# A graph-network layer on one core: edge features and one-hot rows by DMA and ScalarE in place of TensorE, five z banks, all relative targets in one pass

## What is computed

```python
h = jnp.maximum(_layernorm(x, axis=-1), 0.0)
msg_in = jnp.concatenate([h[src], h[dst], edge_attr_32], axis=-1)
messages = act(msg_in @ W1 + b1) @ W2 + b2          # act is x * sigmoid(x)
att_logits = act(msg_in @ Wa1 + ba1) @ Wa2 + ba2
att = jax.nn.softmax(att_logits, axis=0)            # over all edges
messages = messages * att
aggregated = jax.ops.segment_sum(messages, dst, num_segments=6250)
upd_in = jnp.concatenate([h, aggregated], axis=-1)
out = x + act(upd_in @ Wu1 + bu1) @ Wu2 + bu2
```

## Time and profile before

| | |
|---|---|
| median of 3 runs | 2698.34 us (2697.96 to 2699.22) |
| span of the profiled execution | 2700.1 us |
| PE busy (matmul) | 1688.2 us, 63% |
| PE weight loads | 1368.1 us, 51% |
| DVE busy | 1364.4 us, 51% |
| ACT busy | 1064.0 us, 39% |
| POOL busy | 1660.9 us, 62% |
| DMA | 147.93 MB, mean 55 GB/s |
| mean granted TensorE clock | 0.627 of full speed |

### The profile page before, as it was taken

One profiled execution on the slowest core, in us unless ns is written; L12 is line 12 of the kernel. 1 busy time (PEld: TensorE's weight loads), 2 busy tenths in 40 slices (PEclk: granted clock), 3 DMA queues, 4 the chain that ended last, 5 costly groups with the idle time before them and its releaser, 6 DMA issues.

```text
span 2700.1 us, 33245 instructions
## 1 busy us (share of the span) xinstructions
PE 1688.2 (63%) x9168; PEld 1368.1 (51%) x9168; DVE 1364.4 (51%) x2976; ACT 1064.0 (39%) x1875; POOL 1660.9 (62%) x1630
## 2 busy tenths in 40 slices
PE   4366665665766555666666576556666656656668
PEld 3244454554555444554554465445555545545555
DVE  6154444454554445554455554445554445555465
ACT  3244334343434334344334344434344334334342
POOL 4466666566666666666666666666666666666630
PEclk8566667566576666666566655666665666666565
DMA  4221221112222221222222222221222222222200
GB/s 110 70 58 53 56 53 51 51 51 55 54 59 55 54 54 53 54 61 54 55 54 52 55 60 54 55 53 53 55 60 55 54 54 53 55 55 59 52 24 25
DMA packets 122692, 147.93 MB, mean 55 GB/s; under 512 B 66232, under 2 KB 86636, under 8 KB 122668
## 3 DMA queue, kind: packets, MB, share of 16 engines
q0 software_dynamic: 51584, 105.75, 15.1%
q1 hardware_dynamic: 61528, 37.81, 5.3%
q10 hardware_dynamic: 9556, 4.09, 0.5%
HBM read 139.52 MB, written 8.00 MB: 55 GB/s over the span
## 4 chain that ended last, share of the span: by engine, by line
PE 29%; another core or an unknown queue 25%; issue 24%; DVE 13%; ACT 6%; DVEq 1%; ACTq 1%; DMA 1%; SPq 0%
PE bank L631 10%; PE bank L639 8%; DVE s L853 4%; PE bank L615 4%; DVE z L875 2%; DVE z L855 2%; PE ps_prep L595 2%; ACT comb L466 2%; ACT bank L463 2%; PE bank L662 1%; ACT th L485 1%; DVEq L843 1%; PE bank L730 1%; DVE lg L857 1%
## 5 line engine op out<-in xcount | busy, mean ns | idle before, releaser
L374 POOL DMA_INDIRECT p_rows<-p_tab,src_i x1612 | 1640.8, 1018 | 936.1 <-issue 487.5
L631 PE MATMUL bank<-q_win,comb 128*128 128x128 f32 x3224 | 750.8, 396 | 268.8 <-issue 192.0
L631 PEld LDWEIGHTS bank<-q_win,comb 128*128 128x128 f32 x3224 | 656.6, 295 | 354.5 <-issue 257.0
L639 PE MATMUL bank<-hot,v 128*65 128x96 f32 x3224 | 496.8, 302 | 335.2 <-issue 329.1
L463 ACT ACTIVATE bank<-bank,row_no 96x512 f32<-96x512 f32 x403 | 255.9, 648 | 944.8 <-remote 595.6
L639 PEld LDWEIGHTS bank<-hot,v 128*65 128x65 f32 x3224 | 400.4, 177 | 397.1 <-issue 391.1
L853 DVE SCALAR_TENSOR_TENSOR s<-th,z 128x512 f32<-128x512 f32 x403 | 276.3, 686 | 297.4 <-ACT th L485 210.0
L846 DVE SCALAR_TENSOR_TENSOR acc<-acc,fade,bank 65x96 f32 x81 | 25.1, 310 | 743.5 <-remote 579.8
L485 ACT ACTIVATE th<-z 128x512 f32<-128x512 f32 x403 | 253.0, 628 | 260.9 <-DVE z L875 175.1
L875 DVE TENSOR_TENSOR z<-bank,p_rows 128x512 f32<-128x512 f32 x403 | 273.7, 679 | 128.9 <-remote 114.0
L615 PE MATMUL bank<-relT,sel 20*128 20x128 bf16 x1612 | 219.5, 279 | 147.9 <-issue 121.3
(11 more groups left out here) (129 smaller groups left out, 723.8 us busy)
## 6 DMA issues: line engine op xcount, KB each, us to landing
p_rows<-p_tab,src_i POOLq DMA_INDIRECT x1612
ef_sb<-edge_attr SPq DMA_DIRECT2D x80, 320.0 KB
q_win<-q_tab ACTq DMA_DIRECT2D x81, 48.0 KB
p_tab<-th SPq DMA_DIRECT2D x12, 256.0 KB, 2.3
q_tab<-th SPq DMA_DIRECT2D x12, 256.0 KB
x_sb<-x SPq DMA_DIRECT2D x3, 512.0 KB, 5.7
out<-s SPq DMA_DIRECT2D x12, 128.0 KB, 2.0
dst_i<-dst SPq DMA_DIRECT2D x80, 10.0 KB
```

The source lines that it names most:

```text
L374: pool.indirect_dma_start(p_rows[:, a, t * H2:(t + 1) * H2], None, p_tab, bass.IndirectOffsetOnAxis(src_i[:, a, t:t + 1], 0)).then_inc(gat ...
L631: last = nc.tensor.matmul(ps_z[(q + a) % 2][:, (t % TQ) * H2:(t % TQ + 1) * H2], comb[:, a, t * P:(t + 1) * P], q_win[:, a, :], start=True ...
L639: last = nc.tensor.matmul(ps_part[0:U1, 0:WIN], v[:, t, :], hot[:, a, t * WIN:(t + 1) * WIN], start=(t == 0), stop=(t == T - 1))
```

## The change

- The host lays out `src`, `dst` and the features: edge e of a tile lies on partition e (`src.reshape(-1, P).T`), and the features are transposed (`efT`).
- A DMA on SP brings the features straight into the lower 32 rows of `comb`. Another, `load_dst_b`, copies the targets of a group to 96 partitions (`dst_b`, one buffer, 96 x 2560 int32, 983 KB). ACT makes the one-hot by target from it in two parts of 1024 and 1536 columns, `Abs` and `Relu`, both in SBUF. `prepare`, `spread`, `copy_efT`, `copy_relT`, `sel` and `relT` go. The window load moves from ACT's queue to SP's.
- The bank of z is one per quarter (`ps_z = bank[0:5]`); `ps_part`, `ps_small` and the `units` product have banks of their own.
- PE's order for a group is now: the five `zmm` of the next group, each after `add_rows` of the same quarter of this group, then the two matmuls of the maximum, then all 20 of `sums`.
- `rel` of all groups is made once, before `q_rows`; DVE's `window` goes, and the check of the window is done at the start.
- `th` has two slots of a quarter; exp writes the weights into column 64 of `v`; `weigh` and the product of the logits are `scalar_tensor_tensor` (times 1.0) where they were `tensor_tensor`.

```diff
+        def load_window(eng, g, a):
+            node = eng.value_load(base_i[0:1, bass.ds(g, 1)], min_val=0, max_val=N - WIN)
+            eng.dma_start(q_win[0:WIN, a, :], q_tab[bass.ds(node, WIN), :]).then_inc(win_ld[a], 16)
+        def load_ef(eng, g, a, s):
+            T = tiles(g)
+            eng.dma_start(comb[WIN:P, a, 0:T * P], efT[:, bass.ds(g * GE, T * P)]).then_inc(s, 16)
+        def load_dst_b(eng, g):
+            T = tiles(g)
+            eng.dma_start(dst_b[:, 0:T * P], dst_row[:, bass.ds(g * GE, T * P)].broadcast_to([WIN, T * P])).then_inc(dst_b_ld, 16)
...
             def load_group(g, a):
-                wait(sp, prep_done, g - 1)
-                load_edges(sp, g, a, ld[a])
-                if not (isinstance(g, int) and g < 2):
-                    sp.wait_ge(gath[a][NQ - 1], per(a, g - 2, 16 * TQ))
-                load_src(sp, g, a, src_ld[a])
+                nxt, nxt2 = following(g)
+                if nxt is not None:
+                    sp.wait_ge(abs_ok, 2 * g + 2)
+                    load_dst_b(sp, nxt)
+                    wait(sp, z_done, g * NQ)
+                    if not (isinstance(nxt, int) and nxt < 2):
+                        load_ef(sp, nxt, 1 - a, ef_ld[1 - a])
+                    load_window(sp, nxt, 1 - a)
+                if nxt2 is not None:
+                    sp.wait_ge(gath[a][NQ - 1], per(a, g, 16 * TQ))
+                    load_src(sp, nxt2, a, src_ld[a])
...
             def zmm(g, a, q):
                 if q == 0:
-                    pe.wait_ge(efT_ok, g + 1)
+                    pe.wait_ge(ef_ld[a], per(a, g, 16))
                     pe.wait_ge(win_ld[a], per(a, g, 16))
-                wait(pe, z_ok, g * NQ + q - 1)
-                pe.wait_ge(comb_ok, g * NQ + q + 1)
+                wait(pe, z_ok, (g - 1) * NQ + q + 1)
+                if q in (0, 2):
+                    pe.wait_ge(comb_ok, 2 * g + 1 + q // 2)
...
             def group(g, a, units=False):
-                    spread(nxt, 1 - a, [2])
-                    zmm(g, a, 4)
-                    spread(nxt, 1 - a, [3])
-                    zmm(nxt, 1 - a, 0)
-                    spread(nxt, 1 - a, [4])
-                    zmm(nxt, 1 - a, 1)
+                if nxt is not None:
+                    for q in range(tiles(nxt) // TQ):
+                        zmm(nxt, 1 - a, q)
                 pe.wait_ge(pmax_ok, g + 1)
                 nc.tensor.transpose(ps_small[0:1, 0:P], pmax[:], ident[:]).then_inc(maxT_done, 1)
                 pe.wait_ge(gmax_ok, g + 1)
                 nc.tensor.matmul(ps_small[:, 0:1], ones[0:1, :], gmax[:], start=True, stop=True).then_inc(maxB_done, 1)
-                if nxt2 is not None:
-                    prepare(nxt2, a)
-                if nxt is not None:
-                    zmm(nxt, 1 - a, 2)
-                if nxt2 is not None:
-                    spread(nxt2, a, [0, 1])
                 pe.wait_ge(v_ok, g + 1)
                 pe.wait_ge(hot_ok, 2 * g + 2)
                 wait(pe, acc_ok, g)
-                sums(g, a, 0, TG // 2)
-                if nxt is not None and tiles(nxt) > 3 * TQ:
-                    zmm(nxt, 1 - a, 3)
-                sums(g, a, TG // 2, TG)
+                sums(g, a)
...
-                nc.vector.tensor_tensor(parts(z, q)[:, :, U:H2], parts(s2, q)[:, :, U:H2], wa2h[:].unsqueeze(1).broadcast_to([P, TQ, U]), ALU.mult).then_inc(s_sem, 1)
+                nc.vector.scalar_tensor_tensor(parts(z, q)[:, :, U:H2], parts(s2, q)[:, :, U:H2], 1.0, wa2h[:].unsqueeze(1).broadcast_to([P, TQ, U]),
+                                               ALU.mult, ALU.mult).then_inc(s_sem, 1)
...
-                return nc.vector.tensor_tensor(v[:, 0:T, 0:U], s2[:, 0:T, 0:U], ws[:, 0:T].unsqueeze(2).broadcast_to([P, T, U]), ALU.mult)
+                return nc.vector.scalar_tensor_tensor(v[:, 0:T, 0:U], s2[:, 0:T, 0:U], 1.0, w.unsqueeze(2).broadcast_to([P, T, U]), ALU.mult, ALU.mult)
```

More of the change, by code:

```diff
@@ L438, in _ @@
             batches(act, copy_h)
-            def window(g, a):
-                wait(act, z_done, (g - 1) * NQ)
-                node = act.value_load(base_i[0:1, bass.ds(g, 1)], min_val=0, max_val=N - WIN)
-                act.dma_start(q_win[0:WIN, a, :], q_tab[bass.ds(node, WIN), :]).then_inc(win_ld[a], 16)
-            def copy_efT(dst_a, T):
-                for j in range(TQ):
-                    last = nc.scalar.copy(comb[WIN:P, dst_a, 0:T * P].rearrange("p (q j e) -> p q j e", j=TQ, e=P)[:, :, j, :],
-                                          ps_prep[j * DE:(j + 1) * DE, 0:T * DE].rearrange("p (q e) -> p q e", e=P))
-                return last
@@ L469, in _, with one_hot_abs @@
-            stored(act, q_st)
-            act.wait_ge(base_ok, 1)
-            act.wait_ge(const_ok, 8)
-            window(0, 0)
-            copy_relT(0, 0)
-            copy_efT(0, TG).then_inc(efT_ok, 1)
-            for qs in ([0, 1], [2, 3], [4]):
-                one_hots(0, 0, qs)
-            copy_relT(1, 1)
+            HALF = [(0, 2 * TQ * P), (2 * TQ * P, TG * P)]
+            def one_hot_abs(g, a, k):
+                c0, c1 = HALF[k][0], min(HALF[k][1], tiles(g) * P)
+                if k == 0:
+                    act.wait_ge(dst_b_ld, 16 * (g + 1))
+                    wait(act, z_done, (g - 1) * NQ)
+                    act.sem_inc(turn, 1)
+                nc.scalar.activation(comb[0:WIN, a, c0:c1], dst_b[:, c0:c1], ACT.Abs, bias=row_of[0:WIN, bass.ds(g, 1)]).then_inc(abs_ok, 1)
@@ L479, in group, with one_hot_relu @@
+            def one_hot_relu(g, a, k):
+                c0, c1 = HALF[k][0], min(HALF[k][1], tiles(g) * P)
+                act.wait_ge(abs_ok, 2 * g + k + 1)
+                nc.scalar.activation(comb[0:WIN, a, c0:c1], comb[0:WIN, a, c0:c1], ACT.Relu, scale=-1.0, bias=ones[0:WIN, 0:1]).then_inc(comb_ok, 1)
+            act.wait_ge(const_ok, 7)
+            act.wait_ge(rel_ok, 1)
+            for k in range(2):
+                one_hot_abs(0, 0, k)
+                one_hot_relu(0, 0, k)
             def group(g, a, units=False):
-                nxt, nxt2 = following(g)
@@ L606, in spread @@
-            def spread(g, a, qs):
-                T = tiles(g)
-                for q in [q for q in qs if q < T // TQ]:
-                    if q == 0:
-                        pe.wait_ge(relT_ok, g + 1)
-                    wait(pe, comb_ok, g * NQ + q - 1)
-                    pe.sem_inc(turn, 1)
-                    for t in range(q * TQ, (q + 1) * TQ):
-                        last = nc.tensor.matmul(ps_row[(q + a) % 2][:, (t % TQ) * P:(t % TQ + 1) * P], sel[0:T, t, :], relT[0:T, :], start=True, stop=True)
-                    last.then_inc(row_done, 1)
@@ L1052 @@
     from concourse.bass_utils import run_bass_kernel_spmd
+    P = 128
+    GE = EDGE_TILES * P
+    full = N_EDGES // GE * GE
+    last = -(-(N_EDGES - full) // (4 * P)) * 4 * P
+    edges = np.concatenate([np.arange(full), np.arange(N_EDGES - last, N_EDGES)])
+    src, dst, ef = (np.ascontiguousarray(inputs[n])[edges] for n in ("src", "dst", "edge_attr_32"))
+    laid = {
+        "src": src.reshape(-1, P).T,
+        "dst": dst.reshape(-1, P).T,
+        "dst_row": dst.reshape(1, -1),
+        "efT": ef.T,
+    }
+    for name in _INS:
+        laid[name] = inputs[name]
     nc = bacc.Bacc("TRN2", target_bir_lowering=False, num_devices=1)
     arrays, args = {}, []
-    for name in _INS:
-        a = np.ascontiguousarray(inputs[name])
+    for name in ["x", "src", "dst", "dst_row", "efT"] + _INS[1:]:
+        a = np.ascontiguousarray(laid[name])
         arrays[name] = a
```

300 lines of the change are left out of this document (126 added, 174 removed).

## The result

| | before | after |
|---|---|---|
| median, us | 2698.15 (4 runs) | 2651.64 (4 runs) |
| span of the profiled execution, us | 2700.1 | 2645.8 |
| ratio of the times | 1 | 0.983 (95%: 0.981 to 0.985) |

The changed kernel is 1.7% faster; 6.6% was forecast. These are the page's rows of after that answer to the earlier trace rows: busy us, share and instructions by engine, then groups with busy us, mean ns, and idle us before them.

A forecast was written before the change was run, and what follows sets the result against it. POOL's gathers plus stops caused by PE's crawl were taken to bound the kernel. Gathers 25.5 + stops 3.6 = 29.1 us a group; 136 + 78.6 x 29.1 + 99 = 2522, median 2520 us (6.6% less), 8-in-10 range 2230 to 2700.

The forecast's parts named there:

- What bounds the kernel now: Edge groups: 31.3 us each, POOL working 26.4 and stopped 4.9, because PE crawls after some 81 records beside gathers.
- PE's work: PE per group: spreads and transposes go, 110 records become 84, so POOL stops less often.
- m: Groups between two stops of POOL: forecast 1.53, bounds 1 and no stop at all.
- Gathers: POOL's 20 gathers a group: scalar_tensor_tensor for tensor_tensor spares 0.9 us, 26.4 to 25.5; bounds 24.8 and 26.4.
- Stops: POOL's stops: 5.5 us each instead of 4.9, which per group is 3.6 us.
- Head and tail: Before and after the gathering groups: head unchanged at 136 us, give or take 6; tail from 102 to 99.
- ACT, DMAs, banks: ACT's passes, the added dst_b loads (6.1 us a group, covered) and the five z banks: no effect on the time.
- The sum: Whole kernel: 136 + 78.6 groups of 29.1 us + 99 = 2522 us of span, 2520 us median.
- one stop in each group: Rival for POOL: only gathers shrink, 30.4 us a group, 2622 us; chance 0.20.
- Slower: the maximum behind z: Rival at PE: the maximum waits behind 40 records of z, stops grow 5.2 to 10.1 us, 2756 us; chance 0.15.
- It changes nothing: Rival: gathers stay at 26.4 us with one stop of 4.9 a group, 2697 us; chance 0.06.
- POOL never stops: Rival: 84 records stay below what brings the crawl on, only POOL's 25.5 us a group remain, 2237 us; chance 0.17.

The follow-up runs named there:

- tt_back_c: Changed kernel with the logit product and v as tensor_tensor again, on a crawling chip: 2652.7 us, 0.983 of the kernel before.
- after_c: Changed kernel, unaltered, run again on a crawling chip: 2650.9 us, 0.982 of the kernel before.
- tt_back: Changed kernel with the logit product and v as tensor_tensor again, on a chip without the crawl: 2232.0 us, 0.989 of the kernel before.
- w_psum: Changed kernel, ACT writing the weights also into PSUM, where v reads them from group 14 on: 0.983 of before without the crawl (2209.4 us), 0.980 with it (2643.3).
- before_again: Kernel before, unaltered, traced on a chip without the crawl: 2246.0 us.
- after_again: Changed kernel, unaltered, on a chip without the crawl: 2233.5 us, 0.991 of the kernel before.
- max_first: Changed kernel with PE's records of the maximum ahead of the last two quarters of the next group's z, on a crawling chip: 2614.5 us, 0.971 of before.
- late_ahead: Changed kernel, add_part behind the partial maximum, next group's first z added before the wait for the maximum; no crawl: 2278.1 us, 1.008 of before.
- half_sums: Changed kernel without every second tile's sums (64 PE records a group, output wrong), on a chip without the crawl: 2230.3 us.
- pe_more: Changed kernel with 26 more PE records a group, on a chip without the crawl: 2229.5 us, 0.990 of the kernel before.
- hw_rows: Changed kernel with POOL's gathers replaced by plain DMAs of consecutive rows from SP (output wrong), on a chip without the crawl: 1589.7 us.

## Why the prediction was wrong

- *What bounds the kernel now*: right that POOL's 20 gathers and a stop of 4.9 us made the group, that PE's lateness made the stop, and that it ends some 3 us behind the last gather. Wrong in calling it a backlog of **PE's work**, counted in records, of which 84 would nearly all pass. At the place that I read, the wait ended 0.14 us behind the last record of the sums (1509.50 to 1509.64), which looks like arrears; over all 67 such waits of before, 200 to 2400 us, the median is 5.0 us, and 50 are over 2. One row did not show the late messages that the trace had. ACT was not idle in the first of the slow stretches either, as the prediction says: 5.7 of 12.5 us busy.
- *PE's work*, 110 to 84 records, m = 1.53: the step that failed. It took the stop for the time in which PE works off a backlog counted in records, so that fewer records would mean fewer stops. m was 1.05 (78.6 groups, 75 stops; before 78 stops), the 26 records took 0.2 us off a cycle, and the stop ended with a message some 3 us after the last gather. After 78 records PE still crawled, and slower, one record in 2.1 us. Why the message comes then is open. By m = 1 with a stop of 4.9 the sum would have been 136 + 78.6 x 31.3 + 99: no change but in the ends.
- *Gathers*, 25.5 us by the exchange: also failed, 0.9 us a group. The bound "no effect" was the truth (1.018 to 1.014; tt_back_c and after_c alike). The Trainium skill ("SBUF — State Buffer", Who interferes with whom) puts both forms in one class, and the trace agrees. Its statement that `tensor_tensor` does not stall descriptor writing does not hold for these indirect gathers: beside `v` as `tensor_tensor` they took 1.32 and 1.19 us (tt_back), beside the other form 1.20 and 1.19, and with one of its inputs in PSUM 1.01 and 0.94 (w_psum). `L853`, the row that I leaned on, started 0.66 us into its gather; the same instruction does lengthen a gather at whose start it still runs (0.39 us in after_c).
- *Stops*: 5.5 us forecast, 4.8 measured. Per group 3.6 forecast, 4.6 measured (360 us over 78.6 groups): the single stop was put too long, and their number far too low.
- *Head and tail*: 136 and 99 forecast, 132.1 and 94.6 measured, the head inside the 6 us that I gave. *ACT, DMAs, banks* at nothing: right, no wait of ACT for `dst_b` among the large ones.
- *The sum*: of the 124 us between 2522 and 2646, T = 30.8 for 29.1 is +132, head and tail -8. Of T's 1.7 us, 0.7 are gathers with their gaps and short waits (26.2 us a group), 1.0 stops.
- *Rivals*: "one stop in each group" described what happened. It said 2622 us, a span of 2624 for 2646: 55 too low by gathers and short waits, 25 too high by stops, 8 too high by the ends. "Slower: the maximum behind z" had place and order right (`gmax` waits 595.8 us), but it took the place of the stop at `add_part` and did not come on top of it. "It changes nothing" says 2697 us; by its own terms it is 2693. "POOL never stops", 2237 us, is what happens on four of six chips; the changed kernel took 2233.5 us on the one where it ran, a gain of 0.9%. That the times agree is luck: a group took 26.1 us for 25.5, head and tail together 179 us for 235. The trace of before could not show that its main stop belongs to the chip.

## What to carry to other kernels

If an engine stops once per round for a message, reducing the sender's work pays nothing while the message comes at a time set by something else: compare when the waiting engine is let go with what ends just before it, over many rounds, before counting work. A wait ended by "remote" on a single core, and the landing time of the gathers missing from the page (2.5 us in before_again and 2.6 in after_again, none in before and after), were the marks here. Measure a change on more than one chip if its gain rests on a wait of that kind; w_psum gives 0.983 of the kernel before without such a wait and 0.980 with it, where the changed kernel gives 0.991 and 0.982, so its own part shrinks from 0.8% to 0.2%; max_first gives 0.971 with it and was not run without.

## What the runs showed of the hardware

- Of six chips two crawl and four do not, the time of the kernel before being 2692.5 and 2697.8 us on the one kind and 2246 to 2256 us on the other, in all runs on a chip alike. On the crawling kind PE's messages come late: at `add_part` a median of 4.7 us behind the record in after and 0.14 in after_again (7 waits of over 2 us), at the maximum 8.3 us in max_first, where they are let go about 3 us after POOL's last gather.
- The profile itself is thinner there: the page of after has no landing time for `dst_b` (below, after), that of after_again has 7.1 us; the trace of after holds 9,993 updates of semaphores, that of after_again, the same program, 37,379; and the waits at `add_part` are given as "remote". Whatever carries PE's messages seems to carry the trace's events too; that is argued, not shown. The recording of the trace may itself be what holds PE up: every run here was profiled, so whether the crawl would be there without a profiler, and what sets the two kinds of chip apart, stay open.

```profile
dst_b<-dst_row SPq DMA_DIRECT2D x80, 960.0 KB
```

- Not tried on a crawling chip: DVE's new order (late_ahead), fewer or more records (half_sums, pe_more), and rows without POOL (hw_rows). These are the runs that would tell what holds the messages. Nor was a third buffer of rows, which would let POOL run longer between stops and is what the account above asks for.
